# The order of the mixing-weight products, of the first weight roundings and of VectorE's routing copies in a two-layer expert kernel

## The chip, the cores and the metric

The kernel runs on one core of one Trainium2 chip. The metric is the device time of one execution in microseconds (us). The kernel before took 869.05 us, the median of 3 runs (866.9 to 869.88).

## The reference, cut to what matters

Two layers are added onto x, which is [32, 64, 1024] in fp32. Only layer 0 is touched by the change:

```python
h = gelu(embedding @ W0 + b0); h = gelu(h @ W1 + b1)
att = softmax(h @ W2 + b2)                              # 8 mixing weights for each of 32 samples
agg_w = einsum('bk,koi->boi', att, weight)              # one 64 x 64 matrix for each sample
out = einsum('boi,bih->boh', agg_w, x) + (att @ bias_k)[:, :, None]
# for each of the 2048 rows of out: the two best of 8 experts
logits = out @ gate_w;  topv, topi = top_k(logits, 2);  w = softmax(topv)
x = x + sum over the two: w * (out @ expert_w[topi])    # expert_w: 8 x 1024 x 1024
```

Layer 1 is a grouped convolution of 9 taps, a routed low-rank product with a layer norm in its gate, and a dense 1024 x 1024 product.

## The kernel before, in words

All engines run programs written out by hand; semaphores alone tie them together, and the order in each program is the order of its engine. Rows of x are handled in 16 tiles of 128 rows by 1024 columns; stage 1, on which the change acts, goes over them in 8 iterations of two tiles.

Before the iterations, TensorE computes the mixing weights: small products give `att`; `att_t` is its copy spread over partitions (VectorE, L774). The loop at L1214 to L1219 makes the mixed 64 x 64 matrices, 64 matmuls with 8 rows each, from `kern_sb` (loaded at L401) and `att_t` into banks 0 to 3. ScalarE (L660) and VectorE (L788) copy them into the block-diagonal `bd`. Ahead of that loop stand three other products: the column sums of the gate (L1203), the context of layer 1 (L1204) and the spread of `att` for the bias (L1206), and the last two transposes of the first tile pair (`turn_x(0, 2)`, `turn_x(0, 3)`, L1137). Transposes use bank 4 alone, so each waits until ScalarE has taken the one before (`take_turned`, L639). `gate_products(0)` (L1148) needs all four.

In iteration `it`, TensorE runs: `turn_x(it+1, 0)`, `turn_gate(it)` (L1160), two halves of `mix(it, 0)` (L1169), `turn_x(it+1, 1)`, `logits(it)` (L1177), two halves of `mix(it, 1)` with `turn_x(it+1, 2)` between and `turn_x(it+1, 3)` behind, `lists(it-1)` (L1192), `gate_products(it+1)`, `ranks(it)` (L1184, L1185). `logits(it)` waits for `g_sb`, which VectorE writes at L802.

VectorE runs, for each iteration, `take_rows(it)` (L797), `place(it-1)` and `route(it)`. `place` multiplies ranks (L809), reduces them (L811), copies them to `rank_all` (L812) and the expert numbers to `ix_all` (L813), computes `pos_s` (L814), splits it (L816 to L819), copies `g_sb` for the logits (L802, inside `place`), and writes one-hot rows (L831, L832) for `lists`. `route` adds the bias term to the logits (L840), takes maxima and indices, and updates the running count `acc` (L854 to L857). Iterations 2 to 6 are a hardware loop with addresses from registers; 0, 1 and 7 are written out.

ScalarE moves the transposes out of bank 4, the mixed rows out of banks 0 to 3 with their bias (`take_c0`, L648), and at the end of iteration `it` rounds chunk `it` of the first expert's weights to their high part (`round0`, L653). GpSimd then subtracts to get the low part (L530). The chunks pass through two buffers. SyncE loads chunks 0 and 1 at the start. The others it loads one by one, in its own loop:

```python
for it in range(NT // 2):
    for j in range(2):
        sp.wait_ge(s_cev[j], 2 * (it + 1))          # ScalarE has moved out mix(it, j)
        sp.dma_start(c0_d[tile_rows(it * 2 + j), :], c0_sb[j]).then_inc(s_cst[j], 16)
    if it + 2 < HC:
        sp.wait_ge(s_lo, it + 1)                    # GpSimd is done with chunk it
        load_raw0(it + 2)
```

After iteration 7 the row lists are read (L883), the first rows are gathered (L537), and stage 2 multiplies the experts (L1269); stages for layer 1 follow.

Of the kernel before, what the change touches and what calls it, by code (L numbers as in the profile page):

```python
# [7 lines left out]
ALU = mybir.AluOpType  # L8
ACT = mybir.ActivationFunctionType
# [31 lines left out]
QP = P // QUAD  # L41
G_AT, L_AT, R_AT = 0, 2 * E, 4 * E
# [46 lines left out]
def build(nc, x, kern, x_ph, consts_a, consts_b, expert_w, conv_w, down_w, lora_b, out):  # L89
    ctx = ExitStack()  # L90
    with ctx:
        def sb(name, shape, dt=F32):
            return ctx.enter_context(nc.sbuf_tensor(name, shape, dt))
# [106 lines left out]
        rk4 = sb("rk4", [P, 4])  # L200
# [320 lines left out]
        def _(pool):  # L521
            pool.memset(att_rep, 0.0).then_inc(s_init, 1)
            pool.memset(bd[:, :, :], 0.0).then_inc(s_init, 1)
            pool.memset(acc[:, :], 0.0).then_inc(s_init, 1)
# [93 lines left out]
        def _(act):  # L618

            act.wait_ge(s_init, 5)  # L620
            act.activation(warm[:, 0:1], acc[:, 0:1], ACT.Gelu)
# [6 lines left out]
            act.activation(warm[:, 1:2], acc[:, 1:2], ACT.Exp)  # L628
# [26 lines left out]
            for n in range(4):  # L655
                take_turned(0, n)
            act.wait_ge(s_pe0, 7)
            for g in range(QUAD // 2, QUAD):
                for b in range(2):
                    act.activation(*block(g, b), ACT.Copy).then_inc(s_bda, 1)  # L660
            act.wait_ge(s_ctx0, 1)
            act.dma_start(ctx_d, ctx0[:, :]).then_inc(s_ctxd, 16)
            act.wait_ge(s_aggb, 1)
            for it in range(NT // 2):
# [8 lines left out]
                round0(it)  # L673
# [80 lines left out]
        def _(dve):  # L754
# [49 lines left out]
            def place(ch, it, nxt, first=False):  # L804
# [20 lines left out]
            def one_hot(it, first):  # L825
# [4 lines left out]
                for m in range(4):  # L830
                    dve.tensor_scalar(oh_lo[:, m, :], c("iota"), lo_f[:, m:m + 1], None, ALU.is_equal)  # L831
                    ins = dve.tensor_scalar(oh_hi[:, m, :], c("iota"), hi_f[:, m:m + 1],  # L832
                                            c("tok")[:, bass.ds(it * 2 + m // 2, 1)], ALU.is_equal, ALU.mult)
# [636 lines left out]
```

## Time and profile before

| | before |
|---|---|
| median of 3 runs | 869.05 us (866.9 to 869.88) |
| the profiled execution | 863.12 us, its span 861.3 us |
| TensorE matmul busy | 824.4 us (96% of the span) |
| VectorE, ScalarE, GpSimd busy | 407.4, 229.6, 107.4 us |
| stage 1 and what leads to the first gather | 0 to 108 us |
| experts, then layer 1 | 115 us to the end |

The profile is one execution, seen by the hardware profiler. Its page gives busy time by engine, the chain of work that ended last, and groups of instructions. The trace behind it can be asked for single instructions in order of time, for sums over windows, and for transfers with their time from issue to landing. Times count from the start of the span. PE is TensorE, PEld its weight loads, DVE VectorE, ACT ScalarE, POOL GpSimd, SPq the queue of SyncE's transfers. Bracketed text is the idle time in front of an instruction and what ended it.

### The profile page before, as it was taken

What the parts mean: (1) busy time and instruction counts of PE and PEld (TensorE: products, weight loads), DVE (VectorE), ACT (ScalarE), POOL (GpSimd) and SP (SyncE); (2) the same over time, 40 slices, a digit from 0 to 9 for tenths busy, and PEclk for the clock granted to TensorE, in tenths of its full rate; (3) what the DMA queues carried; (4) which work ended last, traced back from release to release, by engine and by line L of the source; (5) the groups of instructions that cost most, each with busy time, mean ns of one, the idle gap of its engine ahead of it and who ended that gap; (6) DMA issues with size and microseconds to landing.
All of it is one profiled execution on the core that took longest, in us unless ns stands there. A gap on an engine that the chain in (4) does not pass through costs nothing.

```text
span 861.3 us, 13429 instructions
## 1 busy us (share of the span) xinstructions
PE 824.4 (96%) x4356; PEld 680.6 (79%) x4357; DVE 407.4 (47%) x944; ACT 229.6 (27%) x359; POOL 107.4 (12%) x145
## 2 busy tenths in 40 slices
PE   6999679999999999999999999999999999999986
PEld 5565468888888888888888888888898889889863
DVE  1577753142333313333133051466666656656597
ACT  2565333142333313333243151310010010001100
POOL 1122221101101001111011112121112111100000
PEclk9999879999999999999999999999999999999999
DMA  8744359655372724727246243575644654630048
GB/s 265 311 170 151 120 210 404 267 179 200 120 257 73 285 92 134 244 78 287 85 157 226 92 167 117 194 242 133 153 105 106 157 127 97 141 78 24 1 127 263
DMA packets 60789, 142.98 MB, mean 166 GB/s; under 512 B 6832, under 2 KB 23488, under 8 KB 60608
## 3 DMA queue, kind: packets, MB, share of 16 engines
q1 hardware_dynamic: 40096, 87.12, 31.1%
q0 software_dynamic: 9968, 36.19, 14.5%
q10 hardware_dynamic: 10704, 19.41, 6.0%
q8 instruction: 11, 0.18, 0.1%
q14 instruction: 10, 0.08, 0.0%
HBM read 94.45 MB, written 39.85 MB: 156 GB/s over the span
## 4 chain that ended last, share of the span: by engine, by line
PE 83%; DVE 6%; DMA 4%; issue 3%; ACT 1%; SPq 1%; DVEq 0%; ACTq 0%; POOL 0%; POOLq 0%
PE bank L1269 62%; PE bank L1308 6%; PE bank L1260 4%; PE bank L1317 4%; PE bank L1169 2%; PE bank L1371 1%; PE bank L1137 1%; DVE work L1111 1%; PE bank L1148 1%; DMA work<-in_expert_w 1%; PE bank L1192 1%; PE bank L1217 1%; DVE rank_all L812 1%; DMA work<-y_scratch,pos_c 1%; DMA x1p<-res 1%
## 5 line engine op out<-in xcount | busy, mean ns | idle before, releaser
L1269 PE MATMUL bank<-weights,l_hi 128*128 128x512 f32 x1696 | 523.6, 390 | 0.0
L1269 PEld LDWEIGHTS bank<-weights,l_hi 128*128 128x128 f32 x1696 | 319.2, 188 | 64.7
L1269 PE MATMUL bank<-weights,l_lo 128*128 128x512 f32 x848 | 335.8, 396 | 1.2 <-DVE l_lo L900 1.1
L1269 PEld LDWEIGHTS bank<-weights,l_lo 128*128 128x128 f32 x848 | 159.7, 188 | 33.4 <-issue 2.3
L900 DVE TENSOR_TENSOR l_lo<-bank,l_hi 128x512 fp32r<-128x512 f32 x37 | 25.6, 693 | 183.6 <-ACT l_hi L679 183.6
L932 DVE TENSOR_TENSOR weights<-work,weights 128x1024 fp32r<-128x1024 f32 x64 | 76.2, 1223 | 50.4 <-ACT weights L690 49.8
L690 ACT ACTIVATE weights<-work 128x1024 fp32r<-128x1024 f32 x64 | 65.1, 1054 | 41.3 <-DMA work<-in_expert_w 23.2
L537 POOL DMA_INDIRECT work<-c_scratch,idx x37 | 41.5, 1122 | 193.6 <-PE bank L1260 192.5
L730 ACT ACTIVATE l_hi<-work 128x512 fp32r<-128x512 f32 x32 | 18.4, 623 | 158.2 <-PE bank L1269 157.5
L1308 PE MATMUL bank<-conv_sb,x1p 128*128 128x128 f32 x512 | 59.8, 275 | 0.4 <-DMA x1p<-res 0.4
L1308 PEld LDWEIGHTS bank<-conv_sb,x1p 128*128 128x128 f32 x512 | 58.8, 192 | 0.7 <-DMA x1p<-res 0.7
L905 DVE TENSOR_TENSOR l_lo<-bank,l_hi 128x512 fp32r<-128x512 f32 x37 | 25.6, 693 | 68.7 <-ACT l_hi L684 68.7
L1045 DVE TENSOR_TENSOR res<-bank,res 128x512 f32 (+1 forms) x32 | 22.0, 689 | 63.4 <-PE bank L1269 63.4
L679 ACT ACTIVATE l_hi<-bank 128x512 fp32r<-128x512 f32 x38 | 22.8, 599 | 95.2 <-PE bank L1269 79.0
L706 ACT ACTIVATE work<-bank 128x512 f32<-128x512 f32 x37 | 21.8, 590 | 94.0 <-PE bank L1269 94.0
L1260 PE MATMUL bank<-ca,work 128*128 128x128 f32 x304 | 40.4, 276 | 5.2 <-DMA work<-c_scratch,idx 5.2
L1260 PEld LDWEIGHTS bank<-ca,work 128*128 128x128 f32 x304 | 36.2, 142 | 10.1 <-issue 5.2
L684 ACT ACTIVATE l_hi<-bank 128x512 fp32r<-128x512 f32 x38 | 22.8, 599 | 74.2 <-PE bank L1269 74.0
L1317 PE MATMUL bank<-down_sb,work 128*128 128x160 f32 x256 | 37.5, 299 | 1.2 <-DVE work L999 1.2
L1317 PEld LDWEIGHTS bank<-down_sb,work 128*128 128x128 f32 x256 | 36.3, 190 | 2.5 <-DVE work L999 1.4
L999 DVE TENSOR_TENSOR work<-bank,ctxb 128x512 f32<-128x512 f32 x32 | 33.9, 1134 | 8.7 <-PE bank L1308 7.8
L585 POOL DMA_INDIRECT work<-y_scratch,pos_c x32 | 32.7, 1023 | 26.3 <-DMA y_scratch<-work 11.1
(178 smaller groups left out, 577.2 us busy)
## 6 DMA issues: line engine op xcount, KB each, us to landing
work<-in_expert_w SPq DMA_DIRECT2D x68, 512.0 KB, 6.3
y_scratch<-work ACTq DMA_DIRECT2D x74, 256.0 KB, 2.1
res<-in_x SPq DMA_DIRECT2D x16, 512.0 KB, 15.4
c_scratch<-work SPq DMA_DIRECT2D x16, 512.0 KB, 3.0
out<-work SPq DMA_DIRECT2D x16, 512.0 KB, 4.3
res<-in_x_ph SPq DMA_DIRECT2D x14, 512.0 KB, 5.6
x1p<-res SPq DMA_DIRECT2D x112, 64.0 KB, 4.7
y_scratch<-ca SPq DMA_DIRECT2D x7, 512.0 KB, 9.3
```

What stands on the lines that cost most here:

```text
L537: pool.indirect_dma_start(xg, None, c0_d, bass.IndirectOffsetOnAxis(ap=idx[:, 0:1], axis=0)).then_inc(s_xg, 16)
L585: pool.indirect_dma_start(yg[j][:, k, :], None, y_d, bass.IndirectOffsetOnAxis(ap=pos_c[j][:, k:k + 1], axis=0)).then_inc(s_yg[j][k], 16)
L679: act.activation(l_hi[:, 0:4, :], bank[2][:, :].rearrange("p (c m) -> p c m", c=4), ACT.Copy).then_inc(s_ha, 1)
L690: act.activation(w_hi[1 - odd][:, half * (HC // 2) + k, :], raw[k], ACT.Copy).then_inc(s_hi, 1)
L900: dve.tensor_tensor(l_lo[:, 0:4, :], bank[2][:, :].rearrange("p (c m) -> p c m", c=4), l_hi[:, 0:4, :].bitcast(F32), ALU.subtract).then_in ...
L905: dve.tensor_tensor(l_lo[:, 4:8, :], bank[3][:, :].rearrange("p (c m) -> p c m", c=4), l_hi[:, 4:8, :].bitcast(F32), ALU.subtract).then_in ...
L932: dve.tensor_tensor(w_lo[1 - odd][:, at, :], raw[k], w_hi[1 - odd][:, at, :].bitcast(F32), ALU.subtract).then_inc(s_lo, 1)
L999: dve.tensor_tensor(out4[:, b], ps, add.unsqueeze(2).to_broadcast([P, CQ, HC, CP]), ALU.add).then_inc(s_c1, 1)
L1260: mm = pe.transpose(bank[bk][:, k * P:(k + 1) * P], xg[:, at * P:(at + 1) * P], ident)
L1269: mm = pe.matmul(to[:, :], a[:, k, :], b[:, k, cols * HALF:(cols + 1) * HALF], start=(k == 0 and n == 0), stop=(k == HC - 1 and n == 2))
L1308: mm = pe.matmul(bank[4 + b][:, at:at + P], x1p[j][:, b, u, m * P + k:(m + 1) * P + k], conv_sb[:, k, u, :], start=(k == 0), stop=(k == WI ...
L1317: mm = pe.matmul(bank[2][:, 0:G1W], c1[:, k, :], down_sb[:, k, :], start=(k == 0), stop=(k == HC - 1))
```

## The change

It has four parts.

1. TensorE makes the mixed matrices (L1214 to L1219) right after `att_t`, ahead of the column sums, the context product, the spread of `att` and the last two transposes of the first pair. ScalarE and VectorE take them first as well. The column sums and the context go to bank 5.
2. VectorE's copies to `rank_all`, `ix_all`, `mx_all` and of `acc` fall away: results are written into slices of the full tensors at once, and the running count is kept as a row of `pre` for every tile.
3. VectorE's hardware loop is written out, with fixed addresses.
4. ScalarE rounds the chunks in the order of `ROUNDS`: chunk 0 after iteration 0, chunks 1 and 2 after iteration 1, 3 after 2, 4 and 5 after 3, 6 after 4, 7 after 5, none after 6 and 7. SyncE's program stays as it is.

```diff
+ROUNDS = [[0], [1, 2], [3], [4, 5], [6], [7], [], []]
...
-        mx = sb("mx", [P, 2, 8])
         ix = sb("ix", [P, 2, 8], U32)
-        mx_all = sb("mx_all", [P, NT, 2])
-        ixf = sb("ixf", [P, 4])
+        mx_all = sb("mx_all", [P, NT, 8])
...
-        pre = sb("pre", [P, 2, E])
-        acc = sb("acc", [P, E])
+        pre = sb("pre", [P, NT + 1, E])
...
-            for n in range(4):
+            for n in range(2):
                 take_turned(0, n)
-            act.wait_ge(s_pe0, 7)
+            act.wait_ge(s_pe0, 5)
             for g in range(QUAD // 2, QUAD):
                 for b in range(2):
                     act.activation(*block(g, b), ACT.Copy).then_inc(s_bda, 1)
+            for n in range(2, 4):
+                take_turned(0, n)
...
                 take_c0(it, 1)
-                round0(it)
+                for k in ROUNDS[it]:
+                    round0(k)
...
             dve.wait_ge(s_pe0, 5)
-            ch.add(dve.tensor_copy(gsum[:, :], bank[2][:, 0:E]))
-            dve.tensor_tensor(ctx0[:, :], bank[3][0:B, 0:CH], c("fside", B), ALU.add).then_inc(s_ctx0, 1)
+            for g in range(QUAD // 2):
+                for b in range(2):
+                    dve.tensor_copy(*block(g, b)).then_inc(s_bdv, 1)
             dve.wait_ge(s_pe0, 6)
+            ch.add(dve.tensor_copy(gsum[:, :], bank[5][:, 0:E]))
+            dve.tensor_tensor(ctx0[:, :], bank[5][0:B, CH:2 * CH], c("fside", B), ALU.add).then_inc(s_ctx0, 1)
+            dve.wait_ge(s_pe0, 7)
             ch.wait()
...
             dve.tensor_reduce(aggb[:, :], aggb_q, AX.X, ALU.add).then_inc(s_aggb, 1)
-            dve.wait_ge(s_pe0, 7)
-            for g in range(QUAD // 2):
-                for b in range(2):
-                    dve.tensor_copy(*block(g, b)).then_inc(s_bdv, 1)
...
-                ch.link(dve.tensor_reduce(rk4[:, :], rk4v, AX.X, ALU.add))
-                ch.add(dve.tensor_copy(rank_all[:, bass.ds(it * 4, 4)], rk4[:, :]))
-                ch.add(dve.tensor_copy(ix_all[:, bass.ds(it * 4, 4)], ixf[:, :]))
-                ch.link(dve.scalar_tensor_tensor(pos_s[:, :], ixf[:, :], float(N), rk4[:, :], ALU.mult, ALU.add))
+                four = slice(it * 4, it * 4 + 4)
+                ch.link(dve.tensor_reduce(rank_all[:, four], rk4v, AX.X, ALU.add))
+                ch.link(dve.scalar_tensor_tensor(pos_s[:, :], ix_all[:, four], float(N), rank_all[:, four], ALU.mult, ALU.add))
...
-                wait_apart(dve, s_chA, ch.base + n)
+                ch.wait(n)
+                mx = mx_all[:, it * 2:it * 2 + 2, :]
                 for j in range(2):
                     n = ch.add(dve.max(mx[:, j, :], lg[:, j, :]))
                 ch.wait(n)
-                ch.add(dve.tensor_copy(mx_all[:, bass.ds(it * 2, 2), :], mx[:, :, 0:2]))
...
-                ch.link(dve.tensor_copy(ixf[:, :].rearrange("p (j k) -> p j k", j=2), ix[:, :, 0:2]))
-                ch.link(dve.tensor_tensor(oh4, iota4, ixf[:, :].unsqueeze(2).to_broadcast([P, 4, E]), ALU.is_equal))
-
-                dve.wait_ge(s_m, it)
-                ch.add(dve.tensor_copy(pre[:, 0, :], acc[:, :]))
+                ixf = ix_all[:, it * 4:it * 4 + 4]
+                ch.link(dve.tensor_copy(ixf.rearrange("p (j k) -> p j k", j=2), ix[:, :, 0:2]))
+                ch.link(dve.tensor_tensor(oh4, iota4, ixf.unsqueeze(2).to_broadcast([P, 4, E]), ALU.is_equal))
+
+                if it > 0:
+                    dve.wait_ge(s_r, it)
                 ch.link(dve.tensor_tensor(msk[:, :, :], oh[:, :, 0, :], oh[:, :, 1, :], ALU.add))
-                ch.link(dve.tensor_tensor(pre[:, 1, :], pre[:, 0, :], msk[:, 0, :], ALU.add))
-                dve.tensor_tensor(acc[:, :], pre[:, 1, :], msk[:, 1, :], ALU.add).then_inc(s_m, 1)
+                ch.link(dve.tensor_tensor(pre[:, it * 2 + 1, :], pre[:, it * 2, :], msk[:, 0, :], ALU.add))
+                dve.tensor_tensor(pre[:, it * 2 + 2, :], pre[:, it * 2 + 1, :], msk[:, 1, :], ALU.add).then_inc(s_m, 1)
+                dve.wait_ge(s_m, it + 1)
...
-            with dve.Fori(2, NT // 2 - 1) as it:
-                ch = Chain(dve, s_chA, (it - 2) * LA + base)
+            for it in range(1, NT // 2):
                 take_rows(it)
-                place(ch, it - 1, it)
+                place(ch, it - 1, it, it == 1)
                 route(ch, it)
...
-            pe.wait_ge(s_init, 5)
+            pe.wait_ge(s_init, 4)
             pe.matmul(bank[6][:, 0:2 * P], bd[:, 0, :], ca[:, 0:2 * P], start=True, stop=True)
             pe.wait_ge(s_att, 1)
             pe.matmul(bank[6][:, 0:B], att_rep, c("ident", B)[:, 0:B], start=True, stop=True).then_inc(s_pe0, 1)
-            pe.wait_ge(s_const, 16)
-            pe.wait_ge(s_gred, 1)
-            pe.matmul(bank[2][:, 0:E], ones, gl[:, :], start=True, stop=True)
-            pe.matmul(bank[3][0:B, 0:CH], c("emb"), c("cw"), start=True, stop=True).then_inc(s_pe0, 1)
-            pe.wait_ge(s_attx, 1)
-            pe.matmul(bank[7][:, B * K8:2 * B * K8], c("ones", B), attx[:, :, :].rearrange("p n k -> p (n k)"),
-                      start=True, stop=True).then_inc(s_pe0, 1)
-            turn_x(0, 2)
-            turn_x(0, 3)
             pe.wait_ge(s_kern, 16 * QUAD)
             pe.wait_ge(s_att, 2)
-            pe.wait_ge(s_ctx0, 1)
...
             mm.then_inc(s_pe0, 1)
+            pe.wait_ge(s_const, 16)
+            pe.wait_ge(s_gred, 1)
+            pe.matmul(bank[5][:, 0:E], ones, gl[:, :], start=True, stop=True)
+            pe.matmul(bank[5][0:B, CH:2 * CH], c("emb"), c("cw"), start=True, stop=True).then_inc(s_pe0, 1)
+            pe.wait_ge(s_attx, 1)
+            pe.matmul(bank[7][:, B * K8:2 * B * K8], c("ones", B), attx[:, :, :].rearrange("p n k -> p (n k)"),
+                      start=True, stop=True).then_inc(s_pe0, 1)
+            turn_x(0, 2)
+            turn_x(0, 3)
             gate_products(0)
```

## Rows read from the trace of the kernel before

**Rows 1.** Windows: PE, PEld, DVE, ACT, POOL busy (instructions), granted clock, DMA share, GB/s.
```profile
44.00:54.00 10.00, 9.56 (x66) 6.17 (x66) 7.84 (x38) 6.16 (x10) 2.35 (x1) 1.00 0.42 162
...
140.00:500.00 360.00, 359.49 (x1707) 299.78 (x1706) 100.35 (x110) 119.09 (x173) 38.44 (x61) 1.00 0.51 179
```

**Rows 2.** Timeline of TensorE, 11 to 26 us: start, duration, instruction, [idle before].
```profile
11.24 0.60 PE L1203 MATMUL bank<-gl,ca 128*128 128x8 f32 x2
...
15.07 1.11 PE L1137 MATMUL bank<-ca,res 128*128 128x128 f32 x4 [0.69 <-ACT work L639]
16.11 7.05 PE L1217 MATMUL bank<-att_t,work 8*128 8x32 f32 x128
...
23.09 1.90 PE L1148 MATMUL bank<-work,ca 128*8 128x256 f32 x16
...
25.12 1.09 PE L1137 MATMUL bank<-ca,res 128*128 128x128 f32 x4
```

**Rows 3.** SyncE's issues; landing of x tiles issued at 3.11 and 5.02; traffic.
```profile
3.59 1.39 SPq L401 DMA_DIRECT2D work<-in_kern  x4
...
res<-in_x SPq DMA_DIRECT2D x1, 512.0 KB, 9.3
...
res<-in_x SPq DMA_DIRECT2D x2, 512.0 KB, 10.7
...
8.00:12.00 4.00, 3.22 (x12) 2.43 (x12) 1.23 (x6) 1.33 (x4) 0.00 (x0) 1.00 0.97 115
12.00:13.00 1.00, 1.00 (x4) 0.50 (x2) 0.28 (x2) 0.00 (x0) 0.00 (x0) 1.00 1.04 233
```

**Rows 4.** Timeline of one loop pass, from ScalarE's weight rounding on.
```profile
43.47 1.06 ACT L653 ACTIVATE weights<-x1p 128x1024 fp32r<-128x1024 f32 x1
...
44.61 2.35 POOL L530 TENSOR_TENSOR weights<-x1p,weights 128x1024 fp32r<-128x1024 f32 x1 [7.14 <-ACT weights L653]
...
44.74 0.60 ACT L639 ACTIVATE work<-bank 128x512 f32<-128x512 f32 x1 [0.21 <-PE bank L1137]
44.98 2.01 DVE L812 COPY rank_all<-rk 128x4 f32 x1
...
46.89 0.60 PE L1137 MATMUL bank<-ca,res 128*128 128x128 f32 x4
...
46.97 0.15 DVE L814 SCALAR_TENSOR_TENSOR pos_s<-ixf,rk 128x4 int32<-128x4 f32 x1
...
47.70 0.17 DVE L802 COPY g_sb<-bank 128x16 f32<-128x16 f32 x1
...
47.93 0.61 PE L1177 MATMUL bank<-g_sb,bd 128*128 128x8 f32 x4 [0.44 <-DVE g_sb L802]
```

**Rows 5.** Timeline at 114 and 121 us: GpSimd's copy beside VectorE's subtractions.
```profile
114.21 0.18 POOL L559 COPY idx<-idx_all 128x1 int32 x1 [4.38 <-issue]
...
120.68 4.63 DVE L932 TENSOR_TENSOR weights<-work,weights 128x1024 fp32r<-128x1024 f32 x4 [1.73 <-ACT weights L690]
...
121.88 1.20 POOL L559 COPY idx<-idx_all 128x1 int32 x1 [5.54 <-DMA work<-c_scratch,idx]
```

**Rows 6.** DMA, us to landing: chunk alone; store behind a chunk; store alone.
```profile
x1p<-in_expert_w SPq DMA_DIRECT2D x1, 512.0 KB, 3.2
...
c_scratch<-work SPq DMA_DIRECT2D x1, 512.0 KB, 3.8
...
c_scratch<-work SPq DMA_DIRECT2D x1, 512.0 KB, 2.6
```

**Rows 7.** Timeline and one window of the last two iterations.
```profile
92.32 2.10 DVE L812 COPY rank_all<-rk 128x4 f32<-128x4 f32 x1
...
100.69 1.79 DVE L812 COPY rank_all<-rk 128x4 f32<-128x4 f32 x1
...
105.15 2.08 PE L1192 MATMUL bank<-work 128*128 128x128 f32 x8 [5.12 <-DVE work L832]
...
101.00:102.00 1.00, 0.00 (x0) 0.00 (x0) 1.00 (x1) 0.00 (x0) 1.00 (x1) 0.62 0.24 90
```

More of the change, by code:

```diff
@@ L523, in _ @@
             pool.memset(bd[:, :, :], 0.0).then_inc(s_init, 1)
-            pool.memset(acc[:, :], 0.0).then_inc(s_init, 1)
+            pool.memset(pre[:, 0, :], 0.0).then_inc(s_init, 1)
             pool.memset(acc2[:, :], 0.0).then_inc(s_init, 1)
@@ L620, in _ @@
             act.wait_ge(s_init, 5)
-            act.activation(warm[:, 0:1], acc[:, 0:1], ACT.Gelu)
+            act.activation(warm[:, 0:1], acc2[:, 0:1], ACT.Gelu)
             act.wait_ge(s_mlp, 16)
@@ L626, in _ @@
             act.activation(h1[:, :], bank[1][:, 0:B], ACT.Gelu, bias=c("b1")).then_inc(s_act0, 1)
-            act.activation(warm[:, 1:2], acc[:, 1:2], ACT.Exp)
+            act.activation(warm[:, 1:2], acc2[:, 1:2], ACT.Exp)
             act.wait_ge(s_sm, 1)
@@ L832, in one_hot @@
                     ins = dve.tensor_scalar(oh_hi[:, m, :], c("iota"), hi_f[:, m:m + 1],
-                                            c("tok")[:, bass.ds(it * 2 + m // 2, 1)], ALU.is_equal, ALU.mult)
+                                            c("tok")[:, it * 2 + m // 2:it * 2 + m // 2 + 1], ALU.is_equal, ALU.mult)
                 ins.then_inc(s_hot, 1)
@@ L839, in route @@
                 for j in range(2):
-                    n = ch.add(dve.scalar_tensor_tensor(lg[:, j, :], gsum[:, :], aggb[:, bass.ds(it * 2 + j, 1)],
+                    n = ch.add(dve.scalar_tensor_tensor(lg[:, j, :], gsum[:, :], aggb[:, it * 2 + j:it * 2 + j + 1],
                                                         bank[5][:, L_AT + j * E:L_AT + (j + 1) * E], ALU.mult, ALU.add))
-                wait_apart(dve, s_chA, ch.base + n)
+                ch.wait(n)
+                mx = mx_all[:, it * 2:it * 2 + 2, :]
                 for j in range(2):
@@ L849, in route @@
                 ch.wait()
-                ch.link(dve.tensor_copy(ixf[:, :].rearrange("p (j k) -> p j k", j=2), ix[:, :, 0:2]))
-                ch.link(dve.tensor_tensor(oh4, iota4, ixf[:, :].unsqueeze(2).to_broadcast([P, 4, E]), ALU.is_equal))
-                dve.wait_ge(s_m, it)
-                ch.add(dve.tensor_copy(pre[:, 0, :], acc[:, :]))
+                ixf = ix_all[:, it * 4:it * 4 + 4]
[3 more added lines that the diff above has]
+                    dve.wait_ge(s_r, it)
                 ch.link(dve.tensor_tensor(msk[:, :, :], oh[:, :, 0, :], oh[:, :, 1, :], ALU.add))
-                ch.link(dve.tensor_tensor(pre[:, 1, :], pre[:, 0, :], msk[:, 0, :], ALU.add))
-                dve.tensor_tensor(acc[:, :], pre[:, 1, :], msk[:, 1, :], ALU.add).then_inc(s_m, 1)
-            LA = 20
+                ch.link(dve.tensor_tensor(pre[:, it * 2 + 1, :], pre[:, it * 2, :], msk[:, 0, :], ALU.add))
+                dve.tensor_tensor(pre[:, it * 2 + 2, :], pre[:, it * 2 + 1, :], msk[:, 1, :], ALU.add).then_inc(s_m, 1)
+                dve.wait_ge(s_m, it + 1)
             take_rows(0)
             take_gate(0)
-            ca0 = Chain(dve, s_chA)
-            route(ca0, 0)
-            take_rows(1)
-            place(ca0, 0, 1, True)
-            route(ca0, 1)
-            base = ca0.n
-            with dve.Fori(2, NT // 2 - 1) as it:
-                ch = Chain(dve, s_chA, (it - 2) * LA + base)
+            ch = Chain(dve, s_chA)
+            route(ch, 0)
+            for it in range(1, NT // 2):
                 take_rows(it)
-                place(ch, it - 1, it)
+                place(ch, it - 1, it, it == 1)
                 route(ch, it)
-                assert ch.n == LA, ch.n
-            ch = Chain(dve, s_chA, base + LA * (NT // 2 - 3))
-            it = NT // 2 - 1
-            take_rows(it)
-            place(ch, it - 1, it)
-            route(ch, it)
-            place(ch, it, None)
+            place(ch, NT // 2 - 1, None)
             dve.wait_ge(s_list, NT // 2)
@@ L1184, in ranks @@
                 pe.matmul(bank[5][:, R_AT:R_AT + 2 * E], c("tri"), msk[:, :, :].rearrange("p j e -> p (j e)"), start=True, stop=False)
-                pe.matmul(bank[5][:, R_AT:R_AT + 2 * E], ones, pre[:, :, :].rearrange("p j e -> p (j e)"),
+                pe.matmul(bank[5][:, R_AT:R_AT + 2 * E], ones, pre[:, it * 2:it * 2 + 2, :].rearrange("p j e -> p (j e)"),
                           start=False, stop=True).then_inc(s_r, 1)
@@ L1248, in _ @@
             pe.wait_ge(s_gev, NT // 2)
-            pe.matmul(bank[4][:, 0:E], ones, acc[:, :], start=True, stop=True).then_inc(s_cnt, 1)
+            pe.matmul(bank[4][:, 0:E], ones, pre[:, NT, :], start=True, stop=True).then_inc(s_cnt, 1)
             for j in range(2):
```

1 line of the change is left out of this document (removed).

## Prediction, made before the changed kernel was run

> **What bounds the kernel now.** I read four views in this order. First the sums by window: from 140 us on TensorE works all the time (359.49 of 360 us in one stretch), and in a pass of stage 1 it is busy 9.56 of 10 us [rows 1]. So whatever moves the end of stage 1 moves the end of the kernel one for one, and inside a full pass at most some 0.5 us can be won, because that is all TensorE leaves idle. Then the timeline of one pass: it shows where the 0.5 us comes from. VectorE's copy to `rank_all`, four numbers wide, takes 2.01 us. It ends at 46.99, and GpSimd's subtraction, which began at 44.61 and took 2.35, ends at 46.96. Behind the copy stand `pos_s`, the splits and `g_sb`; `logits` starts at 47.93, when `g_sb` is there [rows 4]. The same pair shows in the last two iterations (2.10 and 1.79 us), where TensorE has nothing to turn any more and VectorE sets the time [rows 7]. Third, TensorE before the iterations: it is nearly always busy, but part of that is waiting room for a load [rows 2, 3]. Fourth, the transfers, for what SyncE issues when.
>
> **Part 1, the products moved ahead.** `att_t` is there at about 11.5 us, so the products could start there instead of at 16.11. But they also need `kern_sb`. Its four loads are issued from 3.59 to 4.98. The x tile issued before them, at 3.11, lands 9.3 us later, at 12.4. The one behind them, issued at 5.02, lands at 15.7. From 8 to 12 us the transfer engines are full (share 0.97) but move only 115 GB/s, and 233 in the next: this is `kern_sb`, 8 partitions at a time [rows 3]. I take its landing as 13.0, with 12.4 and 15.7 as ends. Then: products 13.0 to 20.0 (7.0). Then the three displaced products, from 11.24 to 13.3 before, 2.05 us: 22.05. Then `turn_x(0, 2)` 1.1, ScalarE's copy 0.65, `turn_x(0, 3)` 1.1, and now also ScalarE's copy of that one, 0.65, which the products hid before and nothing hides now: 25.6. `gate_products(0)` 1.85: 27.4. Before, the next transpose started at 25.12 [rows 2]. That is +2.2 us. Up: +4.9, if the load lands at 15.7. Down: +1.0, if the four transposes, which take 1.11 here and about half of that later, reach the fast level before the gate products. The block copies by ScalarE and VectorE (1.6 and 1.8 us) now lie under the displaced products and cost nothing, and save only 0.1 us of wait. Without that cover they would add 1.8. The bias chain on VectorE ends at about 23.5; its first reader comes after 28. The context's store waits behind two transposes on ScalarE's queue, with nobody waiting for it before layer 1.
>
> **Part 2, the copies dropped.** The copy to `rank_all` is four numbers: by the next copies in the row it is worth 0.08 us. Its other 1.9 us is GpSimd's. The question is whether they go with it. The next instruction, `pos_s`, reads two tensors from SBUF, and behind it stand integer splits and casts from SBUF to SBUF. Of two SBUF inputs the trace shows the reverse case: VectorE's subtractions (1.2 us each) run back to back, and GpSimd's copy between them takes 1.20 us where it takes 0.18 alone [rows 5]. So the two engines exclude each other for such instructions too, and I let `pos_s`, or at the latest the split behind it, wait for GpSimd as the copy did. The wait moves by one instruction. What is left of part 2 in a pass with one subtraction is two copies at 0.08: -0.1 us. Three passes (behind rounding after iterations 0, 2 and, hidden, 3) make -0.2. If nothing behind the copy waited, each would give the 0.5 us that TensorE has idle.
>
> The Trainium skill says so outright. "SBUF — State Buffer", section "Who interferes with whom", has it that an instruction of VectorE with two SBUF inputs contends with a GpSimd instruction that reads SBUF, and that copies, casts and scalar forms can hold the pair of ports that both share, the later one blocking for the whole instruction. By that rule the removed copies save nothing but their own length; by the sum without it each pass would give 0.5 us. The rows at hand agree with the rule as far as they go; none shows `pos_s` itself beside GpSimd.
>
> **Part 3, the loop written out.** Between the reduce and the next start lie 0.33 us in the loop and about 0.1 less outside. This is in VectorE's chain, which has room once the stall is gone: 0. The written-out iterations of before show no fetch stall; the program is longer, so up to +1 in all.
>
> **Part 4, the order of roundings.** Three effects.
>
> (a) After iteration 1 two chunks are rounded. Chunk 2 was loaded long before. GpSimd then subtracts twice in a row, 2.35 us each. `pos_s` gets in between, the split behind it waits for the second. Counting from the start of the rounding T (43.47 in the row), the subtractions run to T+3.5 and T+5.9; `g_sb` comes 0.55 us after the split starts, at T+6.4, and the logits at T+6.6 instead of T+4.46 [rows 4]. +2.1 us; ends -0.1 (the split gets through) and +2.2.
>
> (b) Chunk 5 is wanted after iteration 3, 6 after 4, 7 after 5. But SyncE issues load k only in its iteration k-2, after ScalarE has moved out both tiles of that iteration. That is the moment T itself, since ScalarE rounds right behind `take_c0(it, 1)`. Before, ScalarE came two iterations later. Now: store issued at T, load at T+0.4. A chunk alone lands in 3.2 us. A store right behind a chunk takes 3.8 instead of 2.6 [rows 6], so I add 1.0 for the chunk behind the store: landing T+4.6. Ends: T+3.6 and T+4.8. ScalarE stands still until then, rounds for 1.06, and only then takes the transpose that it took at T+1.3 before (0.6): TensorE can go on with `turn_x(., 1)` at T+6.4 instead of T+3.42 (46.89). The 0.5 us it idled afterwards for `g_sb` is swallowed. Net 3.0 - 0.5 = +2.5 for each of three iterations: +7.4 in all, ends 4.2 (T+3.6) and 8.1. Queued behind the waiting rounding on ScalarE are the transposes, then the mixed rows; TensorE waits for the first of these. GpSimd's subtraction then falls onto VectorE's one-hot rows, which have over 2 us of room before `lists` and `ranks`.
>
> (c) After iterations 5 and 6 no chunk is subtracted during `place(6)` and `place(7)`. Here VectorE is the bound. `place(6)` gains 2.08 (the copy's 2.10 and a following copy, less `pos_s`), `place(7)` 1.77, the dropped copies in `route` 0.16 [rows 7]. Of the first, TensorE holds back 0.5, since mixing and `lists(6)` then come last ahead of `ranks(7)`. -3.5 us; ends -2.6 and -4.6. The lower end is the last `lists`: it takes 2.08 us after 5.1 idle us in which the granted clock fell to 0.5; it fell 1.2 us after TensorE had stopped [rows 7]. If it stays up, 1 us goes.
>
> **The clock.** In (a) and (b) TensorE stands still four times for 2.6 to 2.9 us. A fall came after 1.2 idle us at the end of stage 1 [rows 7]; in a full pass, with 0.5 idle, none came [rows 1]. A fall costs about 1.5 us of work at the half level (1.2 instead of 2.4 GHz). I put one fall into the sum, +1.4; ends 0 and +6.
>
> **Sum.** 2.2 - 0.2 + 2.1 + 7.4 - 3.5 + 1.4 = +9.4 us. On the profiled execution: 863.1 + 9.4 = 872.5. The median of the runs is 5.9 us above that execution, spread over 3 us, for reasons the profile can't show; on the median it is 869.05 + 9.4 = 878.5.
>
> **Rivals.**
> A, faster: the gain at the end decides. If chunks 5 to 7 landed before T+1.7, ScalarE would be in time for TensorE (T+3.42 less 0.65 and 1.06), and all of (b) would go; with `pos_s` free besides, five passes give 0.5 each: 2.2 - 3.5 - 2.5 = -3.8, 865 us. Against it: no landing here is under 2.6 us, and issue comes after T. Chance 0.09.
> B, no change to a little slower: GpSimd holds back nothing behind the copy, chunks land at T+3.6, no fall of the clock: 2.2 - 1.0 + 4.2 - 3.5 = +1.9, 871 us. Chance 0.15.
> C, the clock falls at every stop: +1.4 becomes +6, 883 us. For it: the stops are more than twice the 1.2 us. Chance 0.18.
> My forecast, 874 to 881 us: chance 0.58.
>
> **Range and chances.** 868.5 to 884 holds the forecast, B and C and leaves out A. A measurement can tell 0.3% (2.6 us) from no change. B divides itself: most within, some beyond. Faster 0.09, same 0.12, slower 0.79.
>
> **What would show it.** Part 1: the products at 13 us with a wait for a load in front, the first transpose of iteration 1 at 27.4. Part 2: `pos_s` or the split about 2 us long, ending with GpSimd's subtraction. Part 4: two subtractions in a row near 47 to 52 and `logits` 2 us late; ScalarE idle about 3.5 us three times, released by a transfer of `in_expert_w`; the last two `place` without a stall. I am wrong if the chunks are there at T, or if TensorE has other work in front of that transpose.

## The result, and the profile after

| | before | changed |
|---|---|---|
| median | 868.67 us (866.9 to 869.88, 4 runs) | 879.82 us (874.94 to 883.06, 4 runs) |
| ratio to before | | 1.014, 95% interval 1.0114 to 1.0166 |
| profiled execution | 863.12 us, span 861.3 | 879.60 us, span 877.8 |
| first gather issued | 108.09 us | 121.75 us |
| first large matmul of the experts | 115.22 us | 128.82 us |
| from there to the end of the span | 746.1 us | 749.0 us |

The changed kernel is 1.4% slower, 11.2 us by the medians. The last three rows place the loss: 13.7 of the 16.5 us by which the two spans differ are gone before the first gather, in the stage on which the change acts.

**The start.** The timeline of TensorE of the changed kernel (start, duration, instruction, idle time in front and what ended it) answers to [rows 2]:

```profile
13.42 7.05 PE L1196 MATMUL bank<-att_t,work 8*128 8x32 f32 x128 [2.20 <-DMA work<-in_kern]
...
24.23 1.11 PE L1126 MATMUL bank<-ca,res 128*128 128x128 f32 x4 [0.69 <-ACT work L636]
...
26.04 1.89 PE L1137 MATMUL bank<-work,ca 128*8 128x256 f32 x16 [0.69 <-ACT work L636]
...
27.86 1.12 PE L1126 MATMUL bank<-ca,res 128*128 128x128 f32 x4
```

The products run at 13.42 instead of 16.11 us, but TensorE stood still 2.2 us for the load of `kern_sb` in front of them. Two waits of 0.69 us for ScalarE's copies follow, where there was one. The first transpose of iteration 1 comes at 27.86, 2.7 us later. Another 1.5 us is lost before the logits of iteration 1, and most of it isn't the change's. The first four mixing matmuls run at the low rate here (3.31 us) and ran at the high one in the profile before (1.96 us), but they also took 3.76 us in the kernel with the copies dropped (below), where TensorE's program is that of before:

```profile
26.44 1.96 PE L1169 MATMUL bank<-res,bd 128*128 128x512 f32 x4
```

```profile
26.60 3.76 PE L1156 MATMUL bank<-res,bd 128*128 128x512 f32 x4
```

The first line is of the kernel before, the second of the one with the copies dropped. The granted clock of these windows reads 1.00 in both, so the difference shows only in the durations.

**Two subtractions in a row.** Timelines of GpSimd and VectorE and, in a fence of its own, of TensorE in the changed kernel, pass of iteration 2. It answers to [rows 4], where the copy to `rank_all` took 2.01 us:

```profile
48.87 2.36 POOL L527 TENSOR_TENSOR weights<-x1p,weights 128x1024 fp32r<-128x1024 f32 x1 [7.00 <-ACT weights L650]
51.18 2.34 POOL L527 TENSOR_TENSOR weights<-work,weights 128x1024 fp32r<-128x1024 f32 x1
...
49.14 2.10 DVE L813 SCALAR_TENSOR_TENSOR pos_s<-ix_all,rank_all 128x4 int32<-128x4 f32 x1
51.28 2.27 DVE L815 TENSOR_SCALAR lo_i<-pos_s 128x4 int32<-128x4 int32 x1
```

```profile
54.16 0.61 PE L1166 MATMUL bank<-g_sb,bd 128*128 128x8 f32 x4 [2.40 <-DVE g_sb L802]
```

The copies are gone and `pos_s` takes the 2 us. It ends with the first subtraction. `lo_i`, a split of four integers, then takes 2.27 us and ends with the second. The last line, from TensorE's timeline, is the start of the logits that wait for them, 11.46 us after those of iteration 1 (42.70) where a pass took 9.49.

**Three waits for weights.** ScalarE's roundings with their idle time, SyncE's issues of the chunks they wait for, and the times to landing, all of the changed kernel:

```profile
73.14 1.06 ACT L650 ACTIVATE weights<-x1p 128x1024 fp32r<-128x1024 f32 x1 [3.55 <-DMA x1p<-in_expert_w]
...
86.38 1.06 ACT L650 ACTIVATE weights<-work 128x1024 fp32r<-128x1024 f32 x1 [6.11 <-DMA work<-in_expert_w]
...
100.66 1.06 ACT L650 ACTIVATE weights<-x1p 128x1024 fp32r<-128x1024 f32 x1 [4.43 <-DMA x1p<-in_expert_w]
```

```profile
69.03 0.43 SPq L392 DMA_DIRECT2D x1p<-in_expert_w  x1
...
80.66 1.25 SPq L392 DMA_DIRECT2D work<-in_expert_w  x1
```

```profile
x1p<-in_expert_w SPq DMA_DIRECT2D x1, 512.0 KB, 4.1
...
work<-in_expert_w SPq DMA_DIRECT2D x1, 512.0 KB, 5.7
```

Chunk 5 was issued 0.4 us after ScalarE's last copy of that iteration and landed 4.1 us later; against the 3.2 us of a chunk alone [rows 6] the store in front cost about 1 us. Chunk 6 came later: its issue took 1.25 us instead of 0.33 or 0.43, and it landed after 5.7. This is no accident of one execution. All five profiles with this order of roundings and SyncE's program as it was show a slow issue of chunk 6 (1.18 to 1.50 us), and ScalarE waits 5.24 to 6.11 us for it.

TensorE is held by ScalarE in all three. In the second of these stops the granted clock falls, and again 1.6 us behind the third. Timeline, then windows (PE, PEld, DVE, ACT, POOL busy, granted clock, DMA share, GB/s) of the changed kernel:

```profile
74.74 0.66 PE L1126 MATMUL bank<-ca,res 128*128 128x128 f32 x4 [2.63 <-ACT work L636]
...
87.98 1.12 PE L1126 MATMUL bank<-ca,res 128*128 128x128 f32 x4 [4.24 <-ACT work L636]
...
89.60 2.06 PE L1158 MATMUL bank<-res,bd 128*128 128x512 f32 x2
```

```profile
86.00:87.00 1.00, 0.00 (x0) 0.00 (x0) 0.00 (x0) 0.62 (x1) 0.00 (x0) 0.92 0.00 0
...
90.00:91.00 1.00, 1.00 (x2) 0.31 (x2) 0.90 (x9) 0.00 (x0) 0.00 (x0) 0.50 1.00 406
...
93.00:94.00 1.00, 1.00 (x4) 0.35 (x3) 0.00 (x0) 0.14 (x1) 0.00 (x0) 0.67 0.00 0
```

The clock reads 0.5 (1.2 instead of 2.4 GHz) from 86.8 to 93.7, and two mixing matmuls take 2.06 us that take 1.10 in other passes.

**The last two iterations.** Timeline of the changed kernel; it answers to [rows 7]:

```profile
117.03 0.16 DVE L813 SCALAR_TENSOR_TENSOR pos_s<-ix_all,rank_all 128x4 int32<-128x4 f32 x1
...
119.73 1.16 PE L1181 MATMUL bank<-work 128*128 128x128 f32 x8 [3.43 <-DVE work L831]
```

Without a subtraction beside it `pos_s` takes 0.16 us. TensorE idles 3.43 instead of 5.1 us, and the last `lists` takes 1.16 instead of 2.08. From the last logits to the gather it is 9.02 us instead of 12.73. The pass ahead of these logits shows no gain only because the second fall of the clock (103.9 to 107.3) lies in it: it took 9.98 us, and 8.35 in the second profile of the same kernel (below), where the clock stayed up.

The starts of the logits in iterations 1 to 7 sum this up (us, from the timelines; the column "gather" is the issue of the first gather):

| kernel | 1 | 2 | 3 | 4 | 5 | 6 | 7 | gather |
|---|---|---|---|---|---|---|---|---|
| before | 38.44 | 47.93 | 57.42 | 66.90 | 76.39 | 85.88 | 95.36 | 108.09 |
| changed | 42.70 | 54.16 | 63.50 | 75.23 | 88.89 | 102.75 | 112.73 | 121.75 |
| difference from the column before | +4.26 | +1.97 | -0.15 | +2.24 | +4.17 | +4.37 | +0.50 | -3.71 |

### The profile page after: what moved, and what is told of

The parts are those of the page before. It is cut to its first block, busy times and chain, and to the rows that moved or that the text cites. A ratio compares the mean times of both kernels' runs of the same rounds, so it can differ in the third digit from the quotient of the medians.

```text
span 877.8 us, 13285 instructions
## 1 busy us (share of the span) xinstructions
PE 830.4 (95%) x4356; PEld 683.8 (78%) x4357; DVE 401.6 (46%) x912; ACT 229.0 (26%) x359; POOL 106.8 (12%) x145
## 4 chain that ended last, share of the span: by engine, by line
PE 77%; DMA 8%; DVE 6%; issue 3%; ACT 2%; SPq 2%; ACTq 1%; DVEq 0%; POOL 0%; POOLq 0%
PE bank L1257 56%; PE bank L1296 6%; DMA work<-in_expert_w 4%; PE bank L1305 3%; PE bank L1248 3%; PE bank L1158 2%; PE bank L1126 2%; PE bank L1359 1%; DVE work L1100 1%; DVE weights L921 1%; DMA work<-in_kern 1%; DMA x1p<-in_expert_w 1%; PE bank L1196 1%; DVE pos_s L813 1%; PE bank L1137 1%
## 5 line engine op out<-in xcount | busy, mean ns | idle before, releaser
L1126 PEld LDWEIGHTS bank<-ca,res 128*128 128x128 f32 x128 | 17.8, 167 | 28.6 <-ACT work L636 18.7
```

The costliest lines, as they stand in the source:

```text
L1126: mm = pe.transpose(bank[4][:, k * P:(k + 1) * P], x_sb[t][:, at:at + P], ident)
```

## The experiments

Times are medians; ratios are to the kernel before, run on the same chip, with 95% intervals.

### The parts one by one

**Old rounding order in the changed kernel** (parts 1 to 3 remain):

```diff
-ROUNDS = [[0], [1, 2], [3], [4, 5], [6], [7], [], []]
+ROUNDS = [[0], [1], [2], [3], [4], [5], [6], [7]]
```

> The changed kernel with one chunk rounded after each iteration again, chunk k after iteration k, so parts 1 to 3 of the change are left. My theory: the waits for weight loads and the doubled subtraction go, the early loss of the products stays (the first transpose of iteration 1 at 27.9 us against 25.1, and a later rise of the TensorE clock, +2.7 to +4.3 us), and pos_s waits for GpSimd in all eight iterations as the copy did: +2.5 to +4.5 us against the kernel before. Rival (most of the +11 us is from parts 1 to 3, for instance from the written-out VectorE program): +8 us or more.

Measured: 868.51 us, 1.0011 (0.9998 to 1.0025), +1.0 us. The rival is out: of the loss, all but about 1 us hangs on the order of the roundings. My theory, +2.5 to +4.5 us, was too high; part 1 alone (+2.3 us) and parts 2 and 3 alone (-1.3 us), both below, add up to this +1.0.

**New rounding order alone**, in the kernel before:

```diff
-                round0(it)
+                for k in ROUNDS[it]:
+                    round0(k)
```

> The kernel before with only the order of the first roundings changed (part 4). My theory: ScalarE waits three times for a transfer of the first expert's weights (2 to 6 us each), two subtractions run back to back once, the last two iterations lose their stall; the copy to rank_all shows the 2 us waits, and ix_all or lo_i behind it the second one. +5 to +9 us against the kernel before. Rival (the order of roundings is worth a gain by the free last two iterations): -3.5 us.

Measured: 880.65 us, 1.0154 (1.0121 to 1.0186), +13.4 us, more than expected, and the rival's sign is wrong. In its profile the three waits stand (timeline of ScalarE):

```profile
71.25 1.06 ACT L654 ACTIVATE weights<-x1p 128x1024 fp32r<-128x1024 f32 x1 [3.38 <-DMA x1p<-in_expert_w]
83.91 1.06 ACT L654 ACTIVATE weights<-work 128x1024 fp32r<-128x1024 f32 x1 [5.52 <-DMA work<-in_expert_w]
98.78 1.06 ACT L654 ACTIVATE weights<-x1p 128x1024 fp32r<-128x1024 f32 x1 [4.73 <-DMA x1p<-in_expert_w]
```

and in the pass with two subtractions the copy and, here, `pos_s` behind it wait one after the other (timeline of VectorE):

```profile
47.18 2.01 DVE L814 COPY rank_all<-rk 128x4 f32 x1
49.18 2.31 DVE L816 SCALAR_TENSOR_TENSOR pos_s<-ixf,rk 128x4 int32<-128x4 f32 x1
```

**Products ahead alone**, in the kernel before: the order on TensorE, ScalarE and VectorE of part 1 (the lines of the diff from `take_turned(0, n)` to `s_bdv`, and the block of products on TensorE).

> The kernel before with only the mixing-weight products moved ahead (part 1). My theory: the products wait for their load until about 13.4 us, and gate products stand behind two exposed copies of transposes: the first transpose of iteration 1 at 27.9 instead of 25.1 us; +2.7 us, and up to +4.3 with a later rise of the TensorE clock. Rival (the products ahead take their block copies off the path): 0 or a gain of 0.5 us.

Measured: 869.89 us, 1.0027 (1.0016 to 1.0039), +2.3 us. No gain. Its load landed later still in the profile (timeline of TensorE):

```profile
15.39 7.05 PE L1209 MATMUL bank<-att_t,work 8*128 8x32 f32 x128 [4.07 <-DMA work<-in_kern]
```

**Copies dropped and loop written out alone** (parts 2 and 3; products and roundings as before).

> The kernel before with parts 2 and 3 alone: VectorE's copies dropped and its loop written out, products and roundings as before. My theory: pos_s is 2 us long in every iteration, ending with GpSimd's subtraction; -0.3 to -1.2 us. Rival (the stall belonged to the copy and goes with it): 0.5 us in each of six iterations and 3.5 us in the last two, -6.5 us.

Measured: 865.51 us, 0.9985 (0.9973 to 0.9998), -1.3 us. The rival wanted -6.5. Instructions of one line over the whole span (times in ns, least, median, most):

```profile
L811 DVE SCALAR_TENSOR_TENSOR pos_s<-ix_all,rank_all x8: 1979/2098/2144, 37.5 to 101.6; 128x4 int32<-128x4 f32 x8
```

All eight wait. A pass takes 9.34 instead of 9.49 us; -0.15 in each of eight would be 1.2 us, which fits the -1.3.

Parts 2 and 3 were not run apart, so what the written-out loop does by itself is not shown.

The three parts alone add up to +2.3 - 1.3 + 13.4 = +14.4 us. The changed kernel had 1.014 at first and 1.0188 in a later pair (below), 12 to 16 us: the parts add up within what the runs can tell.

### The lock

The lock is short for VectorE's wait until GpSimd's instruction has ended.

**A small subtraction.** The kernel with the copies dropped, but GpSimd subtracts 16 of 1024 columns:

```diff
-                pool.tensor_tensor(w_lo[0][:, k, :], raw0[k % 2], w_hi[0][:, k, :].bitcast(F32), ALU.subtract).then_inc(s_lo, 1)
+                pool.tensor_tensor(w_lo[0][:, k, 0:16], raw0[k % 2][:, 0:16], w_hi[0][:, k, 0:16].bitcast(F32), ALU.subtract).then_inc(s_lo, 1)
```

GpSimd also clears the low part ahead of its subtractions (lines not shown).

> Products and roundings as before, copies dropped and loop written out (the kernel of the fourth experiment), but GpSimd subtracts only the first 16 of each chunk's 1024 columns; the rest of the low part of the first expert's weights is left out and stands at zero, cleared before the first iteration. So the cost of the lock alone is seen. My theory: pos_s takes 0.16 us in all iterations, six iterations lose about 0.35 us each and the last two 3.5 us together: -5 to -6 us against the fourth experiment, 860 us. Rival (VectorE's wait has another cause than GpSimd): pos_s stays at 2 us and the time does not change.

Measured: 861.27 us, 0.9928 (0.991 to 0.9946), by the ratios 4.9 us below the kernel it is made from, which ran on another chip. Instructions of `pos_s` in it:

```profile
L815 DVE SCALAR_TENSOR_TENSOR pos_s<-ix_all,rank_all x8: 161/161/164, 37.7 to 99.0; 128x4 int32<-128x4 f32 x8
```

2098 ns become 161 when the work of another engine shrinks, with VectorE's program untouched. That the 2 us are GpSimd's is shown. The passes go from 9.34 to 9.17 us, 0.17 instead of the 0.35 expected. The logits no longer wait for `g_sb` there, so TensorE is the bound.

### The transfers

**Loads in time.** The changed kernel, with SyncE's loads moved ahead of the stores of an iteration:

```diff
+            LOADS = [[], [2], [3, 4], [5], [6], [7], [], []]
             for it in range(NT // 2):
+                for k in LOADS[it]:
+                    sp.wait_ge(s_lo, k - 1)
+                    load_raw0(k)
                 for j in range(2):
...
-                if it + 2 < HC:
-                    sp.wait_ge(s_lo, it + 1)
-                    load_raw0(it + 2)
```

> The changed kernel, with SyncE loading each chunk of the first expert's weights as soon as its buffer is free, ahead of the stores of that iteration, instead of behind them. All else as changed. My theory: the three waits of ScalarE for a chunk (3.6, 6.1 and 4.4 us) go, and with them the two falls of the TensorE clock in them; left are the double subtractions (now two, +2 us each), the early loss and the gain at the end: -9 to -12 us against the changed kernel, so 867 to 871 us. Rival (the waits are not the cost, the doubled subtractions and their lock are): -3 us at most, 876 us.

Measured: 876.09 us, 1.010 (1.0077 to 1.0123), between the two theories and nearer to the rival's 876: 3.5 us below the changed kernel by its first ratio (1.014), 7.6 us by its second (1.0188, below). In its profile ScalarE waits for no transfer any more, and the gather is issued at 112.92 instead of 121.75, 8.8 us earlier. So the waits are what the late loads cost, but I had undervalued what remains: now both pairs of chunks are subtracted back to back, and in this profile each costs a stop of TensorE and a fall of the clock behind it (timeline and windows of this kernel):

```profile
52.25 0.74 PE L1166 MATMUL bank<-g_sb,bd 128*128 128x8 f32 x4 [2.41 <-DVE g_sb L802]
74.69 0.61 PE L1166 MATMUL bank<-g_sb,bd 128*128 128x8 f32 x4 [2.40 <-DVE g_sb L802]
```

```profile
53.00:54.00 1.00, 1.00 (x2) 0.48 (x3) 1.00 (x6) 0.00 (x0) 0.00 (x0) 0.50 0.62 201
...
77.00:78.00 1.00, 1.00 (x2) 0.19 (x1) 0.89 (x7) 0.41 (x1) 0.00 (x0) 0.50 0.00 0
```

A fall does not follow such a stop each time: in the changed kernel none came behind the 2.40 us at 54.16. The profiled execution is also the fastest of the six runs, which lie from 871.66 us (mean granted clock 0.985) to 878.08 (0.982), so the 8.8 us overstate the gain.

**The kernels' load first**, in the kernel with the products ahead: the four loads of `kern_sb` are issued before `load_x(1)` instead of behind it.

> Products ahead as in the third experiment, and the four loads of the kernels for the mixing weights issued ahead of x tile 1 instead of behind it. My theory: the load lands at about 9 to 11 us, the products start at 11.4 us, 2 us or more earlier than in the third experiment; the exposed copy of the last transpose stays, so the result is +0.3 to +1.0 us against the kernel before. Rival (the order on TensorE loses by itself, whatever the load): +2 us or more, as in the third experiment. Another (the freed order wins): below the kernel before.

Measured: 869.19 us, 1.0016 (1.0001 to 1.0031), +1.5 us. The products still waited:

```profile
12.37 0.94 PEld L1209 LDWEIGHTS bank<-att_t,work 8*128 8x128 f32 x16 [1.30 <-DMA work<-in_kern]
```

The products started at 12.37 us, not at the 11.4 that I had put. That is earlier than in every profile without the swap, where the load ended such a wait between 13.06 and 17.43 us. The order stays a small loss, +0.1 to +2.7 us, and this interval rules out neither my theory nor the rival. Between the two kernels, +2.3 and +1.5, the intervals overlap, so a gain of the swap is not shown.

### The clock

**Matmuls in the waits.** Run twice; the second time beside the changed kernel on the same chip.

```diff
+                if it in (4, 5, 6):
+                    pe.wait_ge(s_cev[1], it * 2)
+                    for f in range(5):
+                        pe.matmul(bank[2][:, 0:256], bd[:, it * 2, :], ca[:, 0:256], start=True, stop=True)
                 if not last:
                     turn_x(it + 1, 1)
```

> The changed kernel, with five more matmuls of 128 by 256 on TensorE in each of iterations 4, 5 and 6, where it otherwise stands still for ScalarE's copy; their results go to bank 2 and are overwritten. My theory: TensorE works through the first 2 us of each wait, the granted clock no longer falls there, and the passes after the waits are 1.5 us shorter each where it fell: -2 to -4 us against the changed kernel. Rival (the fall costs nothing beside the waits, or comes all the same): no change or up to +1 us.

> The changed kernel as it stands, beside the next one on the same chip, to settle whether the falls of the clock in the waits cost time of their own. My theory: 878 to 881 us; falls of the granted clock to 0.5 in the waits of two or three of the four long stops.

> The changed kernel with five more matmuls in each of iterations 4, 5 and 6, as before. My theory: no fall in these three waits, and 2 to 4 us below the changed kernel on the same chip. Rival (the falls cost nothing of their own in the sum, since TensorE's slower passes take the place of waits): within 1 us of it.

Measured: first 878.56 us, 1.0121 (1.0096 to 1.0146); then 881.04 us, 1.0177 (1.0156 to 1.0198), beside 882.43 us, 1.0188 (1.0156 to 1.0219), for the changed kernel. That second time of the changed kernel missed its expectation (878 to 881 us), and its profile shows one fall of the clock in the long stops, not two or three. In the filled kernel's profile no fall came in these three waits. With the matmuls, and without:

```profile
87.00:88.00 1.00, 0.38 (x3) 0.38 (x4) 0.00 (x0) 1.00 (x3) 0.84 (x1) 1.00 0.00 0
```

```profile
89.00:90.00 1.00, 1.00 (x7) 1.00 (x6) 0.00 (x0) 0.90 (x2) 1.00 (x1) 0.50 0.00 0
```

and the gather is issued at 117.63 instead of 121.49. All five profiles that have the three waits for weights tell the same. The column "three passes" is the time from the logits of iteration 3 to those of iteration 6, beyond the 28.46 us of the kernel before:

| kernel | three passes | falls in or behind the three waits |
|---|---|---|
| new rounding order alone | +10.63 us | 2 |
| changed, first profile | +10.79 us | 2 |
| changed, second profile | +10.74 us | 1 |
| matmuls in the waits, first | +6.92 us | 0 |
| matmuls in the waits, second | +7.54 us | 0 |

ScalarE waits as long in both kernels of the pair (13.49 and 13.55 us in all), so the 3.2 us between +10.74 and +7.54 are what one fall of 6.8 us cost. In each unfilled profile the fall of the chunk 6 wait is of that length; a second one, of 3.4 us, lies mostly in the pass behind.

The timed runs show only 1.3 and 1.4 us, within their intervals, too little for my theory and too much for the rival. Their mean granted clocks say why the profiles show more. The filled kernel's profiled execution of the pair is its fastest (874.39 us) and has 0.990; the other five have 0.982 to 0.988 and take 880 to 883 us. So the clock falls in those too; at which places can't be seen. The same order holds within every kernel with these stops: the new rounding order alone runs from 876.09 us at 0.986 to 884.32 at 0.978, the changed kernel from 874.94 at 0.987 to 883.06 at 0.981 and, the second time, to 886.53 at 0.979. The kernel before stays at 0.986 to 0.989. About 1 us goes with each 0.001. By that estimate the changed kernel's means of 0.984 and 0.982, against 0.988 before, stand for some 4 to 6 of its 12 to 16 us. This goes by how the two move together; no run holds the clock up throughout.

### A faster version

**Two chunks ahead.** Copies dropped, products as before. ScalarE rounds chunks 0 and 1 before the first iteration and one chunk after each of iterations 0 to 5, with the loads issued to match:

```diff
+ROUNDS = [[2], [3], [4], [5], [6], [7], [], []]
...
             act.wait_ge(s_aggb, 1)
+            for k in range(2):
+                round0(k)
...
+            for k in range(2, 4):
+                sp.wait_ge(s_lo, k - 1)
+                load_raw0(k)
...
-                if it + 2 < HC:
-                    sp.wait_ge(s_lo, it + 1)
-                    load_raw0(it + 2)
+                if it + 4 < HC:
+                    sp.wait_ge(s_lo, it + 3)
+                    load_raw0(it + 4)
```

> Copies dropped and loop written out, products as before, and chunks 0 and 1 rounded before the first iteration, when both have landed, then one chunk after each of iterations 0 to 5, with loads 2 and 3 issued behind the x tiles and each later one two iterations ahead of its use. My theory: GpSimd's subtractions before the iterations fall on slack of VectorE, no iteration has two, and place(6) and place(7) are free: -3.5 us against the fourth experiment, 862 us, faster than both kernels. Rival (chunk 2 lands too late behind the x tiles and holds ScalarE in iteration 0): a wait of 2 us or more there, 864 us or slower.

Measured: 862.56 us, 0.9945 (0.993 to 0.996). The gain at the end is there. Both theories had a part in it, since chunk 2 did hold ScalarE (timeline of ScalarE):

```profile
38.77 1.06 ACT L653 ACTIVATE weights<-work 128x1024 fp32r<-128x1024 f32 x1 [2.12 <-DMA work<-in_expert_w]
```

**Chunks earlier.** The same, with the two roundings placed in front of ScalarE's wait for the products:

```diff
             for n in range(4):
                 take_turned(0, n)
+            for k in range(2):
+                round0(k)
             act.wait_ge(s_pe0, 7)
```

> As the kernel with two chunks rounded ahead, but ScalarE rounds chunks 0 and 1 already while TensorE makes the mixing weights, ahead of its block copies, so that GpSimd frees the first buffer at about 21 us and load 2 goes out right behind the x tiles. My theory: the 2.1 us wait of ScalarE for chunk 2 in iteration 0 and the late store credit behind it go: -1 to -2 us against that kernel, 861 us. Rival (load 2 queues behind the x tiles and lands as late): no change. Another (GpSimd's subtraction of chunk 1 now holds VectorE's block copies): later gate products, +1 us.

Measured: 862.71 us, 0.9954 (0.9939 to 0.9968). That wait is gone (ScalarE now waits 0.93 and 2.79 us for chunks 0 and 1 before the iterations) and the passes run at 9.34 us from the first, as expected; the gather is issued at 105.42 instead of 106.15. The medians show no difference. So the 1 to 2 us expected did not come; by the issue of the gather 0.7 was in it. Either version is about 0.5% faster than the kernel before: part 2 of the change, and the idea of part 4 with loads that keep up and no doubled subtraction.

## Why the prediction was right

It said 878.5 us, 868.5 to 884, and slower; 879.82 was measured. The mechanisms were right at nearly every step, but that the time came out so close is partly luck. The sum has +9.4 us; the ratio of 1.014 is +12.2 (9.9 to 14.4), the later one of 1.0188 is +16.3, and that later median, 882.43 us, lies in the range but outside the forecast of 874 to 881. What hid this is the base: the 869.05 us of 3 runs stand above the medians of later runs of the same kernel (867.39, 867.72, 867.14 and 866.63 us, 11 to 29 runs each, on several chips).

Up to the first gather the profiles differ by 13.66 us, 4.3 more than the sum. Of these, 2.1 lie ahead of the logits of iteration 1, and 2.0 in the three passes with late loads and the fall of the clock (+10.8 instead of 7.4 + 1.4).

- **Part 1, +2.2 us.** The load was put at 13.0 us and ended the wait at 13.42; the first transpose of iteration 1 was put at 27.4 and came at 27.86. Alone, the part costs 2.3 us. The 4.26 us at the logits of iteration 1 hold 1.35 us more for mixing matmuls at the low rate, which the kernels without part 1 show as well. The gain that I kept as an end (transposes at the fast level before the gate products) did not come: they took 1.1 us each.
- **Part 2, the wait moves on.** Right at each step: `pos_s` is 2.1 us long in the four iterations of the changed kernel with a subtraction beside it, and in all eight of the kernel with the copies dropped; `lo_i` waits behind it in the doubled case, and nothing waits without GpSimd. The Trainium skill's rule, from "SBUF — State Buffer", section "Who interferes with whom", was weighed against a sum of 0.5 us for each pass, and the rows of `pos_s` and of `lo_i` agree with it: both kinds of instruction that it names waited. The saving of a pass was 0.15 instead of 0.1 us (and three passes at 0.1 make 0.3, not the 0.2 of the sum).
- **(a) Doubled subtraction, +2.1 us.** +1.97 in the pass. I counted it once; with loads in time it comes twice.
- **(b) Late loads, 3 x 2.5 us.** The mechanism, its place and its size were right: landing T+4.6 was forecast and chunk 5 ended ScalarE's wait at T+4.6 (68.52 to 73.14). Without a fall of the clock, in the two filled profiles, the three passes grew by 6.9 and 7.5 us where I had 7.4. Two misses cancel in this: the pass of chunk 5 grew by 2.24 and not by 2.5, and chunk 6 came later than the end T+4.8 in every profile (T+6.1 in the changed kernel, T+5.2 at the earliest), since its issue was slow. Chunk 7 came at T+4.4.
- **(c) The last two iterations, -3.5 us.** From the logits of iteration 6 to the gather it took 19.00 instead of 22.21 us, -3.2, with the second fall of the clock in it and with the last `lists` at the high level, the way that I had kept as an end. In the second profile, with no fall before the last logits and `lists` at 1.91 us, it is -4.1. The table's -3.71 is the part behind the last logits.
- **The clock, +1.4 us for one fall.** This is the term that was mis-sized. The work at the low level was put at 1.5 us for a fall; the fall in the wait for chunk 6 lasted 6.8 us in all three unfilled profiles and cost 3.2 in the pair, and two of the three had a second one. Part 4 alone costs 13.4 us (10.5 to 16.1), and my terms for it, (a) to (c) and the clock, give 7.4. Its mean clock of 0.982 against 0.988 stands for about 6 us by the estimate above, which leaves about 7 for (a) to (c), where I had 6.0.
- **The base.** The 5.9 us between profiled execution and median could not be read then. The other profiles show where most of it lies: from the first large matmul to the end the profile before took 746.1 us, the other thirteen between 747 and 751, whatever the change. Part of that is the clock, which stays low for 3.1 us behind the first large matmul in the profile before and for 5.8 in that of the changed kernel, an estimated 1.3 us of work. And the logits of iteration 1, with TensorE's program unchanged, stood at 40.42 us in the kernel with the copies dropped instead of 38.44, as the first four mixing matmuls ran at the low rate there; no other profile with the old order of products has these logits before 40.1. So the profiled execution was a lucky one, and the 16.5 us between the two spans overstate the change.

The rivals: A fell on the loads (T+4.4 at best, T+1.7 needed); B on `pos_s` and on chunk 6; C, 883 us, is nearer than its chance of 0.18 said: the profiles have one or two falls at four stops, of 3.2 and about 1.6 us where C put 1.5 for each, and the second median of the changed kernel is 882.43.

## What to carry to other kernels

When a tiny instruction takes microseconds and ends with an instruction of another engine, removing it hands the wait to the next one in line; look at what kind that is before counting the gain, and move the other engine's work instead. When work is pulled forward, follow its input back to the queue that issues the load: here the rounding moved and the load did not, and the engine that waited held another behind it. A gain that is real at one end (3 to 4 us) can be kept by paying for it elsewhere in slack; the version with two chunks ahead did that. And when a kernel makes TensorE stop, compare the mean granted clocks of its runs, not only the times: one profiled execution can be the luckiest of its kind.

## What the hardware showed beside this

- The issue of a chunk of 512 KB on SyncE in the iterations took 0.33 to 0.43 us in most cases, but 1.25 us for chunk 6 in the changed kernel, and between 1.0 and 1.5 us for one or two of these loads in the profiles of five experiments (the new order alone, the loads in time, and the three runs about the clock). Where the load stands behind the stores, it was chunk 6 each time, and chunk 4 as well in the three runs about the clock. Chunk 6 landed late (5.7 us in the changed kernel, against 4.1 and 4.0 of chunks 5 and 7). In the kernel before, no chunk had it. What causes it was not tried.
- The landing of `kern_sb`, loaded into 8 partitions at a time, scatters: it ended TensorE's wait between 13.06 and 17.43 us in eight profiles with the same issues in front of it. At 17.43 (the kernel with two chunks ahead) it held the products back even in their old place.
- With two subtractions of GpSimd back to back, one four-element instruction of VectorE ended with the first (51.24 and 51.23 us) and the next with the second (53.55 and 53.52).
